# Moving the bias sum of the offsets ahead of chunk 7's convolution groups, and the norm of x1 behind the selections of chunk 5

## The reference

```python
x1  = x + mix @ depthwise3x3(gn(x))            # mix = G . pointwise . A, 32x32, from softmaxes
off = conv3x3(gn(x1), w_off)                   # 64 offset channels: rows and columns
xd  = bilinear(gn(x1), grid + off)             # per channel, four neighbours
out = x1 + conv3x3(xd, w_conv) + b_conv
```

## Time and profile before

| what | value |
|---|---|
| median of 3 runs | 899.59 us |
| the profiled execution, its own time | 901.44 us |
| its span | 899.5 us |
| granted TensorE clock, mean | 0.923 |
| PE busy | 751.7 us, 84% |
| VectorE busy | 548.5 us, 61% |
| GpSimd busy | 478.9 us, 53% |
| ScalarE busy | 440.5 us, 49% |
| HBM read and written | 16.91 and 16.78 MB |

### The profile page before, as it was taken

How to read it: one execution, slowest core, us unless ns; L and a number is a source line. 1 busy time by engine, 2 the same in 40 slices (tenths; PEclk the granted TensorE clock), 3 DMA queues, 4 the chain that set the end, 5 groups by cost and what they waited for, 6 DMA issues and landing times. The chain is left out here.

```text
span 899.5 us, 9213 instructions
## 1 busy us (share of the span) xinstructions
PE 751.7 (84%) x2780; PEld 298.2 (33%) x2780; DVE 548.5 (61%) x1064; ACT 440.5 (49%) x781; POOL 478.9 (53%) x401
## 2 busy tenths in 40 slices
PE   3864697699979998899979997999889999579154
PEld 2321233333334332434333332433233433223021
DVE  6374259856984589466955698458946675435211
ACT  0112566477435844566527643575456556545000
POOL 0002475688456746576636755674647766676200
PEclk9978799899989999899979998999979999789678
DMA  8298225959777959677875877796965257523254
GB/s 151 44 187 141 53 48 103 201 111 186 151 136 162 175 105 190 161 141 137 181 144 125 167 148 144 165 169 115 193 156 120 65 127 164 123 51 94 62 128 96
DMA packets 218439, 119.58 MB, mean 133 GB/s; under 512 B 144560, under 2 KB 210192, under 8 KB 214288
## 3 DMA queue, kind: packets, MB, share of 16 engines
q1 hardware_dynamic: 193040, 106.35, 58.5%
q10 hardware_dynamic: 25344, 12.59, 8.3%
HBM read 16.91 MB, written 16.78 MB: 37 GB/s over the span
## 5 line engine op out<-in xcount | busy, mean ns | idle before, releaser
L1010 DVE COPY_PREDICATED other_row<-down_ps,row_diff 128x768 f32<-128x768 int32 x128 | 123.6, 1019 | 211.0 <-ACT down_ps L682 211.0
L534 PE MATMUL off_ps<-x1a,wo 128*128 128x512 f32 x384 | 201.3, 664 | 13.8 <-DVE other_row L1022 7.7
L825 POOL TENSOR_TENSOR other_row<-other_row,x_quads 128x512 f32<-128x512 f32 x64 | 75.9, 1186 | 254.9 <-DVE other_row L1022 254.6
L453 PE MATMUL c_ps<-mapb,w 128*64 128x512 f32 (+1 forms) x384 | 169.4, 592 | 31.8 <-DMA mapb<-mapa 31.8
L453 PE MATMUL c_ps<-xb,w 128*64 128x512 f32 (+1 forms) x384 | 171.5, 595 | 17.4 <-ACT xb L591 17.4
L455 PE MATMUL c_ps<-xa,w 128*64 128x512 f32 x384 | 177.4, 610 | 0.0
L534 PE MATMUL off_ps<-x1b,wo 128*128 128x512 f32 x384 | 176.2, 595 | 0.0
L455 PE MATMUL c_ps<-mapa,w 128*64 128x512 f32 x384 | 175.3, 607 | 0.0
L811 POOL TENSOR_TENSOR row_diff<-x_quads 128x594 f32<-128x594 f32 x64 | 79.1, 1237 | 91.5 <-ACT x_quads L707 91.5
L673 ACT ACTIVATE other_row<-row_diff 128x768 f32<-128x768 f32 x128 | 101.7, 843 | 40.6 <-POOL row_diff L811 30.4
L534 PEld LDWEIGHTS off_ps<-x1a,wo 128*128 128x128 f32 x384 | 74.5, 207 | 115.0 <-issue 97.5
(11 more groups left out here) (103 smaller groups left out, 813.6 us busy)
## 6 DMA issues: line engine op xcount, KB each, us to landing
xb<-xa SPq DMA_DIRECT2D x32, 520.0 KB, 8.8
x1b<-x1a SPq DMA_DIRECT2D x32, 520.0 KB, 6.4
mapb<-mapa SPq DMA_DIRECT2D x32, 520.0 KB, 8.8
mapa<-mapped SPq DMA_DIRECT2D x256, 64.0 KB, 2.6
out_dram<-x1a SPq DMA_DIRECT2D x56, 256.0 KB, 4.7
x_quads<-x1a SPq DMA_DIRECT2D x192, 65.0 KB, 2.2
xa<-in_x_dram ACTq DMA_DIRECT2D x48, 256.0 KB, 5.5
xa<-in_x_dram SPq DMA_DIRECT2D x16, 256.0 KB, 6.4
```

The source lines that it names most:

```text
L453: nc.tensor.matmul(bank[0:64, n0:4 * W], weights[:, kx, :], rows_b[:, b0:4 * g + 4, kx:kx + W], start=(kx == 0), stop=(kx == 2))
L534: last = nc.tensor.matmul(off_ps[k % 2][:, CH * n:CH * n + CH], wo[wpar][:, kx, :], rows[:, 4 * k:4 * k + 4, kx:kx + W], start=(kx == 0), ...
L825: step(pool.tensor_tensor(split(column), split(column), own, ALU.add))
L1010: last = dve.copy_predicated(other_row[n][:, :, KR // 2 * odd:KR // 2 * odd + KR // 2, :], bass.AP(tensor=rows.tensor, offset=rows.offset ...
```

## The change

Three things are changed. The job "bo" moves from the end of chunk 7 to the place behind chunk 7's offsets, ahead of the c2 groups 5, 6 and 7. Its result goes to one of two tiles `bias_o`, by the parity of the image, so that it can be written while the other one is in use; ScalarE writes it behind `sum_far` of chunk 7 and no longer behind the pads and the clamp of the next image, and its waits for users of the tile now name an image further back. And VectorE's `x1_norm` moves from ahead of the selections of chunk 5 to behind them.

```diff
+    NEXT_BIAS = 7
...
             jobs += [("x1", i + 1, m) for m in NEXT_CONV1[k]]
+            jobs += [("bo", i + 1, 0)] if k == NEXT_BIAS else []
         if i >= 1:
             jobs += [("b2", i - 1, 0)] if k == CONV2_SETUP else []
             jobs += [("c2", i - 1, m) for m in (LAST_CONV2 if i + 1 < NB else END_CONV2)[k]]
-        if i + 1 < NB and k == NK - 1:
-            jobs += [("bo", i + 1, 0)]
...
-        bias_o = sb("bias_o", [P, 1])
+        bias_o = [sb(f"bias_o{n}", [P, 1]) for n in range(2)]
...
-            def offset_biases(i, ps):
-                if not (isinstance(i, int) and i == 0):
-                    act.wait_ge(parts_ready, NK * i)
-                    act.wait_ge(off_used, NK * i)
+            def offset_biases(i, par, ps):
+
+                served = max(i - 1, 0) if isinstance(i, int) else i
+                if not (isinstance(i, int) and served == 0):
+                    act.wait_ge(parts_ready, NK * served)
+                    act.wait_ge(off_used, NK * served)
                 act.wait_ge(bo_summed, i + 1)
-                act.activation(bias_o[:, 0:1], ps[:, 0:1], ACT.Copy, scale=-1.0).then_inc(bo_ready, 1)
+                act.activation(bias_o[par][:, 0:1], ps[:, 0:1], ACT.Copy, scale=-1.0).then_inc(bo_ready, 1)
...
                     if k == 1:
                         clamp(i, 1)
+                    if nxt and k == NEXT_BIAS:
+                        offset_biases(i + 1, (i + 1) % 2, bank("bo", i + 1, 0))
                 if nxt:
                     pad_x1(i + 1, (i + 1) % 3, 0)
                     clamp(i + 1, 0)
-                    offset_biases(i + 1, bank("bo", i + 1, 0))
...
                 for k in range(NK):
-                    if k == X1_NORM and nxt:
-                        x1_norm(i + 1, (i + 1) % 2, (i + 1) % 3)
                     if k == CONV2_SETUP and prev:
                         prepare_conv2(i - 1, (i - 1) % 3)
...
                     deform(i, k)
+                    if k == X1_NORM and nxt:
+                        x1_norm(i + 1, (i + 1) % 2, (i + 1) % 3)
```

More of the change, by code:

```diff
@@ L682, in offset_parts @@
                 act.activation(down_ps[:, :], off_ps[n][:, 0:2 * CH:2], ACT.Relu,
-                               bias=bias_o[:, 0:1]).then_inc(parts_ready, 1)
-                act.activation(off_abs[n][:, :], off_ps[n][:, :], ACT.Abs, bias=bias_o[:, 0:1]).then_inc(abs_ready, 1)
+                               bias=bias_o[i % 2][:, 0:1]).then_inc(parts_ready, 1)
+                act.activation(off_abs[n][:, :], off_ps[n][:, :], ACT.Abs, bias=bias_o[i % 2][:, 0:1]).then_inc(abs_ready, 1)
                 act.wait_ge(abs_ready, g + 1)
                 act.activation(off_ps[n][:, 1:2 * CH:2], off_ps[n][:, 1:2 * CH:2], ACT.Relu,
-                               bias=bias_o[:, 0:1]).then_inc(cols_ready, 1)
+                               bias=bias_o[i % 2][:, 0:1]).then_inc(cols_ready, 1)
             def sum_far(i, k):
@@ L718, in _ @@
             pad_x1(0, 0, 1)
-            offset_biases(0, bank("bo", 0, 0))
+            offset_biases(0, 0, bank("bo", 0, 0))
             clamp(0, 0)
@@ L763, in _ @@
                     pad_x1(v, 0, 1)
-                    offset_biases(v, c_ps[2])
+                    offset_biases(v, 0, c_ps[2])
                     act.wait_ge(bo_ready, v + 1)
@@ L770, in _ @@
                             d = off_ps[k % 2][:, a:2 * CH:2].rearrange("p (h w) -> p h w", h=KR)
-                            last = act.activation(coord[:, a, :, :], d, ACT.Identity, bias=bias_o[:, 0:1])
+                            last = act.activation(coord[:, a, :, :], d, ACT.Identity, bias=bias_o[0][:, 0:1])
                         last.then_inc(off_used, 1)
@@ L1018, in deform @@
                 dve.copy_predicated(other_row[n][:, 0, :, :], cols, other_row[n][:, 2, :, :]).then_inc(col_selected, 1)
-                step(dve.scalar_tensor_tensor(own, down, bias_o[:, :], own, ALU.add, ALU.mult))
+                step(dve.scalar_tensor_tensor(own, down, bias_o[i % 2][:, :], own, ALU.add, ALU.mult))
                 dve.wait_ge(col_selected, g + 1)
                 settle()
-                dve.scalar_tensor_tensor(beside, down, bias_o[:, :], beside, ALU.add, ALU.mult).then_inc(off_used, 1)
+                dve.scalar_tensor_tensor(beside, down, bias_o[i % 2][:, :], beside, ALU.add, ALU.mult).then_inc(off_used, 1)
             def bank(*job):
```

## The result

The changed kernel takes 931.40 us, the median of four runs (929.59 to 932.29), against 897.73 us for the kernel before in the four runs that it is compared with. The ratio is 1.0364, with a 95% interval of 1.0330 to 1.0398: slower by 33.7 us, where 29.4 had been forecast.

What follows compares the result with a forecast made beforehand. Two nearly equal loops were taken to bound the kernel: TensorE's through "bo", and VectorE to SyncE to `mapb` to c2 group 0. Terms 21.4, clock 3 and GpSimd 5 gave +29.4 us on 899.59, so 929, range 905 to 942.

Steps and rivals of the forecast that it cites:

- The gap in front of the sum goes, and a gap opens at "b1": TensorE's 6.43 us gap before "bo" and 1.5 us slow clock go; a gap opens one chunk later, behind VectorE.
- "bo" and group 7's wait for the bias cost nothing: Chunk 7 on TensorE: bias ready at 548.6, group 7 asks at 550.6, covered by 2 us; no cost.
- The norm's move makes the selections of 7 end 5.1 us later, against T5: VectorE: idles before chunk 5's selections, then the norm delays selections of 6 and 7 by 5.1 us.
- GpSimd's company: VectorE's moved norm: GpSimd, busy beside it, slows its operations by 0.8 us for six images, +5 us.
- The loop through SyncE and `mapb`: SyncE issues 5.1 us later, so c2 group 0 waits for `mapb` 3 to 6 us in images 1 to 5.
- images 1 to 5, stalls at c2 group 0: TensorE at c2 group 0: new 4.2 us stall for `mapb`, +3.7 us for each of four images.
- slow clock behind the stalls: TensorE's matmuls after the five new stalls run at low clock: 0.6 us taken each, +3 us.
- image 6 to the end, group 4's bank: Image 6, chunk 6: group 4 waits for its bank until group 1's sum behind the norm, +1.5 us once.
- the gap is really won (888): Rival: selections of 6 and 7 do not slip, TensorE's gap is truly saved, 888 us; chance 0.12.
- the terms cancel (900): Rival: VectorE's slip and the room before `mapb` is needed cancel, no change, 900 us; chance 0.11.
- Rival D: Chunk 7: group 7 waits for the bias, 1 to 3 us an image; no own chance, counted inside the main forecast.
- rival E: GpSimd holds every such operation in the moved norm: 20 us in place of 5, 944 us; chance 0.07.

## Why the prediction was right, point by point

*The gap in front of the sum goes, and a gap opens at "b1".* Right. The gap at "b1" was said to come from VectorE; it is 3.0 us at the longest.

*"bo" and group 7's wait for the bias cost nothing.* Right: TensorE has no wait for `bias_o` in its list, and the kernel with only the sum's move has no wait in chunk 7. The cover of 7 us between the norm and "bo" isn't there in image 0, which has no c2 groups. Three rows of TensorE from its step to image 1:

```profile
158.52 1.41 PE L502 MATMUL c_ps<-mean,wo 128*128 128x1 f32 x6 [4.37 <-DVE wo L979]
...
180.59 4.87 PE L534 MATMUL off_ps<-x1a,wo 128*128 128x512 f32 x6 [3.80 <-DVE other_row L1025]
...
226.47 0.48 PE L453 MATMUL c_ps<-mapb,w 128*64 128x384 f32 x1
```

"bo" waits 4.37 us for `wo`. It does no visible harm: the next offsets wait for ScalarE's `x1b` anyway and start at 166.74, where they started at 167.22.

*The norm's move makes the selections of 7 end 5.1 us later, against T5.* Right in mechanism and size, before GpSimd's company is added: 5.1 in image 4 (39.9 against 34.8), and 4.6, 4.0, 5.1, 5.1 and 4.4 in images 1 to 5. The norm itself became 0.9 us longer (550.95 to 560.7, against 519.05 to 527.9). The rule of the Trainium skill ("SBUF — State Buffer", "Who interferes with whom") can be read in this row beside the 1.24 us multiplication at 556.38 above:

```profile
556.35 1.26 POOL L840 TENSOR_TENSOR mapped<-other_col,other_row 128x512 f32<-128x512 f32 x1
```

GpSimd's operation starts 0.03 us ahead and both end at 557.6; of the three multiplications one took 1.24, one 0.69 and one 0.15 us. The second, at 558.12, ended with GpSimd's next operation (557.57 to 558.81), and the third, at 559.33, met none. So the trace agrees with the rule; the upper bound of three held ones came of taking GpSimd as busy through the whole norm. The selections of 6 were therefore 6.0 us late, but those of 7 only 5.1: the norm of x between them took 8.4 us (572.70 to 581.1) instead of 9.3 (544.47 to 553.7), since GpSimd no longer held one of its multiplications for 1.02 us. That gave back what the moved norm had cost, and was not foreseen.

*The loop through SyncE and `mapb`.* Right for images 2 to 5: 42.8 us from release to last copy, as before, and stalls of 4.09, 5.22, 4.19 and 4.05 us where 4.2 was reckoned. Wrong for image 1, where 3 to 6 us were forecast as well: group 0 starts at 226.47 with no wait, as the third row above shows, and even the old 0.97 us is gone. TensorE itself gets there later, 83.1 us behind T5 of image 0 instead of 76.7. Its first lasting delay is the second row above: the offsets of chunk 1 wait for VectorE's late selections of chunk 7. Then ScalarE's clamp starts at 200.16, where it started at 195.72. So the 5.0 us of this step hit the forecast 5.1, but they came by VectorE's and ScalarE's hold on TensorE and not by `mapb`; which part each has isn't shown. That the kernel before had next to no slack there is shown by the sum's move alone, which won nothing in images 1 to 5. Why the way is that long was not seen; it was put down to issuing, and the queue's content is more of it.

*The sum of terms.* By T5, against the trace of before:

| step | forecast, us | measured, us |
|---|---|---|
| image 0 to 1 | 5.1 | 5.0 |
| images 1 to 5, stalls at c2 group 0 | 4 x 3.7 = 14.8 | 15.5 |
| slow clock behind the stalls | 3 | 8.0 |
| GpSimd's company | 5 | within the 15.5 |
| image 6 | 0 | -0.4 |
| image 6 to the end, group 4's bank | 1.5 | 2.6 |
| sum | 29.4 | 30.7 |

The measured steps of images 1 to 5 are 413.6 - 390.1 = 23.5 us together; 8.0 of it is the slow clock (10.66, 10.54, 11.76 and 10.65 against 8.91 each), the rest stands in the line of the stalls, with GpSimd's part in it. That rest is VectorE's lateness in images 1 to 4, 4.6 + 4.0 + 5.1 + 5.1 = 18.8, less 3.3 of room: before the change the last `mapb` copy had landed 0.4 to 1.8 us ahead of group 0 in images 2 to 5. In the forecast it was 4 x 5.1 = 20.4, less 5.6. The 2.6 us from image 6 on are the later T7 of image 6, 23.9 us behind its T5 instead of 21.3. So the terms mis-sized are the clock, taken at 0.6 a stall where 1.6 to 2.9 was measured in four of the five, and GpSimd's company, taken at 5 where the two norms together show almost none. They nearly cancel, and the total is right partly by that luck; the hit in the step to image 1 is luck as well.

*The rivals.* That the gap is really won (888) and that the terms cancel (900) both failed on VectorE's row without a gap, which the norm's move alone shows: +31 us. Rival D did not occur, and rival E (944) neither: VectorE would have been up to 3.3 us later still. Not separated by any run: how the queue's stiffness divides between `x1b`, the loads of a further image and the quads' small pieces.

## What to carry to other kernels

When an engine waits for something at a fixed place, ask first whether the next transfer or sum would have been there had it not waited: here a 6.4 us gap, five times, was worth 5 us in all, the earlier copy behind it 3, and the two together 28. Small work that fills an engine's idle time is free only there; moved past the work that ends the idle time it cost 31 to 38 us here wherever that engine's end bound the loop, and 10 where it did not. And the issue time of a DMA is not its own cost alone: here a store that took three times as long to issue as its twin had a megabyte ahead of it.

## What the runs showed of the hardware

- What stands ahead in a DMA queue lengthened the issuing of what came next. With the megabyte of `x1b` ahead of them, three stores took 5.90 us to issue, and when they were taken away, the quads behind took 1 us each instead of 0.7; with `x1b` sent 14 us earlier the stores took 2.58.
- A wait of 4 to 5 us on TensorE cost 1.6 to 2.9 us more in matmuls at the low clock, and nothing when four fp32 matmuls filled it. The length of the wait alone does not decide: with `x1b` sent early, 3.46 us of waiting in image 5 left the clock at 1.00, and with the sum's move beside it 2.52 us in image 5 brought it to 0.50 and cost 1.7. The waits of 2.4 us for group 4's bank were in some images followed by slow matmuls and in others not: in the changed kernel T7 lies 13.3 us behind T6 in images 1, 2, 4 and 6 and 15.0 in images 3 and 5.
- An fp32 matmul of 512 columns stands in the trace as two records of 0.43 us start to start. Two matmuls that write different halves of a bank's partitions, one from `xb` and one from `xa`, started within 0.01 us of each other, and the next pair 0.43 us later, so that a pair cost no more than one.
